# The lag between two lanes of a megakernel: from almost in step to a third of a turn

## The reference

```
x += tanh(g_xattn[0]) * attention_16_heads(layernorm(x), ctx)            # A0
x += tanh(g_ffn[0])   * moe_8_experts_top2_plus_2_shared(layernorm(x))   # M0
x += tanh(g_xattn[1]) * attention_16_heads(layernorm(x), ctx)            # A1
x += tanh(g_ffn[1])   * switch_head_attention(layernorm(x))              # SW, 16 heads, 8 value experts, top 2
x += tanh(g_xattn[2]) * mlstm(layernorm(x), ctx, ctx)                    # ML, 4 heads
x += tanh(g_ffn[2])   * bitlinear_conv_ffn(layernorm(x))                 # CF, 512 hidden
x += tanh(g_xattn[3]) * attention_1_head_with_ffn(layernorm(x), ctx)     # WA
x += tanh(g_ffn[3])   * moe_16_experts_top4_plus_shared(layernorm(x))    # M3
```

## Time and profile before

| what | value |
|---|---|
| median of 3 runs | 2666.93 us (2659.13 to 2669.15) |
| profiled execution, its own time | 2663.77 us |
| its span, first to last instruction | 2661.8 us |
| mean granted TensorE clock | 0.975 |
| PE, DVE, ACT, POOL busy | 89%, 60%, 54%, 5% of the span |
| instructions | 53043 |
| DMA | 115.28 MB, mean 43 GB/s |

### The profile page before, as it was taken

The page is one execution under the profiler, slowest core; times in us unless marked ns, Lnnn a source line. Parts: engine busy times, 40 slices in busy tenths (PEclk is TensorE's granted clock), DMA queues, the critical chain, the costliest instruction groups (busy, mean ns, idle before and its releaser), DMA issues.

```text
span 2661.8 us, 53043 instructions
## 1 busy us (share of the span) xinstructions
PE 2380.6 (89%) x20418; PEld 1673.0 (63%) x20418; DVE 1597.2 (60%) x5337; ACT 1448.7 (54%) x4482; POOL 140.6 (5%) x180
## 2 busy tenths in 40 slices
PE   5999889998899989999899998999889998899998
PEld 3667556675566755667565775557665576665766
DVE  3754766546666475664755657556475565755656
ACT  4376364763647536475455744558345583455833
POOL 0000100001000010000000000000000000000010
PEclk9999999999999999999999999999999999999999
DMA  3024000340003300043000420005200051000510
GB/s 153 1 62 115 9 13 1 76 101 17 5 1 89 88 17 5 1 102 75 17 5 1 112 65 17 5 1 113 63 17 5 1 131 46 18 3 6 141 30 5
DMA packets 312299, 115.28 MB, mean 43 GB/s; under 512 B 268736, under 2 KB 295360, under 8 KB 311792
## 3 DMA queue, kind: packets, MB, share of 16 engines
q1 hardware_dynamic: 312048, 111.90, 16.7%
HBM read 63.64 MB, written 48.23 MB: 42 GB/s over the span
## 4 chain that ended last, share of the span: by engine, by line
PE 52%; DVE 22%; ACT 16%; issue 5%; DMA 3%; POOL 2%; SPq 0%; DVEq 0%; ACTq 0%
ACT PP L821 7%; PE banks L463 5%; PE banks L344 4%; PE banks L407 4%; PE banks L293 3%; PE banks L503 3%; PE banks L574 2%; ACT PP L829 2%; PE banks L341 2%; PE banks L680 2%; DVE nm L1165 2%; PE banks L355 2%; DVE qk L1236 1%; PE banks L456 1%; PE banks L547 1%
## 5 line engine op out<-in xcount | busy, mean ns | idle before, releaser
L821 ACT ACTIVATE PP<-banks,nm 128x128 f32<-128x128 f32 x1568 | 495.7, 419 | 138.8 <-DVE nm L1165 96.1
L1165 DVE TENSOR_REDUCE nm<-banks 128x4 f32<-128x512 f32 (+1 forms) x400 | 261.4, 675 | 323.9 <-PE banks L344 279.2
L293 PE MATMUL banks<-identb 128*128 128x256 bf16 x2112 | 339.6, 277 | 19.1 <-ACT PP L829 15.6
L293 PEld LDWEIGHTS banks<-identb 128*128 128x128 bf16 x2112 | 195.7, 100 | 130.2 <-ACT PP L829 53.9
L407 PE MATMUL banks<-w_sb,PP 128*128 128x128 f32 x1536 | 243.5, 283 | 37.1 <-ACT PP L829 22.4
L829 ACT ACTIVATE PP<-banks 128x512 f32<-128x512 f32 (+1 forms) x400 | 250.9, 638 | 46.9 <-PE banks L407 31.6
L1684 POOL TENSOR_TENSOR mv<-mv,half 128x2 f32<-128x2 f32 x160 | 112.4, 702 | 2339.5 <-DVE mv L1062 2339.5
L407 PEld LDWEIGHTS banks<-w_sb,PP 128*128 128x128 f32 x1536 | 173.0, 143 | 87.8 <-ACT PP L829 49.7
L463 PE MATMUL banks<-w_sb,qk 128*128 128x128 f32 x1280 | 190.8, 287 | 9.0 <-ACT qk L1043 9.0
L463 PEld LDWEIGHTS banks<-w_sb,qk 128*128 128x128 f32 x1280 | 161.1, 191 | 38.1 <-issue 11.4
L812 ACT ACTIVATE xnT<-banks 128x256 f32<-128x256 f32 x128 | 49.1, 384 | 211.4 <-PE banks L301 211.4
(11 more groups left out here) (281 smaller groups left out, 4408.9 us busy)
## 6 DMA issues: line engine op xcount, KB each, us to landing
va<-v_d SPq DMA_DIRECT2D x32, 512.0 KB, 4.8
o_d<-oa SPq DMA_DIRECT2D x64, 256.0 KB, 3.3
va<-o_d SPq DMA_DIRECT2D x32, 512.0 KB, 4.5
pv_d<-PP SPq DMA_DIRECT2D x32, 256.0 KB, 2.0
oa<-pv_d SPq DMA_DIRECT2D x32, 256.0 KB, 3.3
v_d<-PP SPq DMA_DIRECT2D x16, 512.0 KB, 3.8
v_d<-tmp SPq DMA_DIRECT2D x16, 512.0 KB, 6.2
w_sb<-weights SPq DMA_DIRECT2D x1, 5603.0 KB, 23.6
```

Source lines behind the costliest of these rows:

```text
L293: pe.matmul(bank(k, n)[:, cols(c, T)], identb[:, :], bc(identb[:, :], 1, G), start=True, stop=True, skip_group_check=True)
L821: e = act.activation(P[k][:, 512 * (u % 2) + 128 * j:][:, 0:128], bank_[:, cols(j)], ACT.Exp, bias=nm[k][:, m:m + 1], accum_out=ssum[k][:, ...
L1165: e = dve.tensor_reduce(m, b3(scores[:, 0:maps * 128], maps), AX.X, ALU.max, negate=True)
```

## The change

TURN goes from 36496 to 34943 and SHIFT from 1318 to 11636: the keys of lane 1 lie 0.333 of a turn behind lane 0's, where they were 0.036 behind. All five lists of beats and the list of spares have new values; their lengths are the same. The sum of the spares goes from 132 to 212, the entries that aren't zero from 39 to 48, and the largest from 8 to 15. The beats of SyncE now run from -31436 to 692. Of the lists of PE and ACT the first two rows are shown.

```diff
--- before.py
+++ after.py
@@ -34,49 +34,49 @@
 A0, M0, A1, SW, ML, CF, WA, M3 = range(8)
 
 
-TURN, SHIFT = 36496, 1318
+TURN, SHIFT = 34943, 11636
 BEATS_PE = (
-    -398, 99, 355, 606, 918, 1233, 1233, 1786, 2057, 2088, 2276, 2372, 2720, 2741, 3250, 3264, 3271, 3435, 3831, 3923, 3923,
-    3923, 4446, 4727, 4831, 4831, 4939, 5512, 5780, 5780, 5780, 5885, 6047, 6158, 6220, 6327, 6444, 6798, 7066, 7301, 7484,
...
+    -262, 372, 372, 1316, 1447, 1889, 2018, 2182, 2238, 2442, 2657, 2657, 2707, 2743, 2743, 3178, 3442, 3737, 3922, 3986,
+    3996, 4036, 4066, 4348, 4410, 4474, 4576, 4826, 4826, 4826, 5060, 5632, 6143, 6143, 6547, 6910, 6976, 7097, 7119, 7324,
...
 BEATS_ACT = (
-    -80, -80, -80, 205, 616, 662, 1324, 1324, 1324, 1796, 2178, 2483, 2483, 2483, 2752, 3172, 3172, 3339, 3511, 4116, 4245,
-    4621, 5108, 5283, 5681, 5724, 5782, 5792, 5792, 6169, 6358, 6509, 6591, 6747, 7220, 9035, 9225, 9460, 9618, 9717, 9903,
...
+    438, 1172, 1216, 1587, 1596, 1706, 2102, 2121, 2264, 2264, 2421, 2421, 2480, 2480, 2684, 3263, 3673, 3673, 3956, 3956,
+    4204, 4204, 4893, 4943, 4984, 4984, 5121, 5260, 5260, 5913, 5913, 6499, 6536, 6646, 8122, 8955, 8968, 9376, 9483, 9483,
...
 BEATS_DVE = (
-    -1050, -180, -180, 486, 658, 1436, 1436, 2572, 2592, 3007, 3599, 4639, 4765, 5192, 5192, 5254, 5932, 5998, 6096, 6126,
-    6126, 6285, 6360, 6360, 6428, 6542, 6542, 6679, 6972, 6972, 6972, 6972, 6972, 6972, 6972, 7211, 7250, 7895, 7895, 7895,
-    7895, 7895, 8032, 8077, 8330, 8636, 8768, 9040, 9196, 9466, 9556, 10430, 10636, 10966, 11150, 11982, 12252, 13019,
-    13337, 13694, 13694, 14180, 14180, 14180, 14180, 14180, 14180, 14180, 14180, 14180, 14180, 14180, 14578, 14981, 14981,
-    15393, 15602, 15776, 16374, 16575, 16946, 17050, 17050, 17087, 17125, 17218, 17428, 17510, 17605, 17758, 17800, 17800,
-    17800, 18210, 18298, 18453, 18464, 18583, 18583, 18583, 19143, 19162, 19681, 19738, 20426, 20459, 20641, 22259, 22553,
-    23220, 23488, 23672, 23709, 23804, 24103, 24542, 24664, 24664, 24862, 25392, 25548, 25639, 26058, 26179, 27284, 27605,
-    27639, 27712, 28230, 28230, 28272, 28390, 28436, 28911, 29245, 29245, 29587, 29762, 29977, 31316, 31997, 32051, 32158,
-    32664, 32816, 33291, 33408, 33408, 33408, 33468, 33488, 33547, 33798, 34058, 34185, 34313, 34324, 34621, 34908, 34983,
-    35032, 35080, 35217, 35300, 35492, 35539, 36135,)
+    -1150, -262, -262, 355, 377, 1449, 1607, 1810, 1911, 2843, 2908, 3494, 3719, 3752, 3843, 4237, 4915, 4947, 5088, 5147,
+    5147, 5210, 5356, 5412, 5439, 5439, 5445, 5844, 5901, 6138, 6138, 6221, 6524, 6524, 6543, 6543, 6808, 6848, 6848, 7013,
+    7026, 7180, 7358, 7358, 7384, 7557, 7900, 7951, 8741, 9416, 9426, 9714, 9820, 10833, 10936, 11552, 11761, 12264, 12264,
+    12800, 12985, 13181, 14026, 14111, 14144, 14345, 14345, 14345, 14367, 14714, 14714, 14780, 14780, 14780, 14780, 14780,
+    14910, 15664, 16356, 16426, 16489, 16845, 16913, 16915, 17011, 17092, 17156, 17424, 17424, 17440, 17440, 17440, 17472,
+    17472, 17608, 18133, 18434, 18728, 18824, 19115, 19268, 19818, 20375, 20375, 20707, 20887, 20961, 22660, 23017, 23017,
+    23259, 23523, 23523, 23523, 23538, 24321, 24321, 24616, 24964, 25071, 25166, 25479, 25904, 25904, 26527, 26786, 26786,
+    26786, 26935, 26963, 28052, 28054, 28054, 28357, 28510, 28546, 28747, 29899, 29914, 30799, 30999, 31135, 31201, 32195,
+    32461, 32461, 32577, 32584, 32584, 32735, 32834, 32834, 32956, 33016, 33027, 33483, 33483, 33483, 33483, 33666, 33666,
+    33794, 33794, 34096, 34228, 34228, 34838,)
 BEATS_POOL = (
-    18722, 24380, 28829, 30432, 32719, 39274, 39274, 40884, 48435, 51418, 51418,)
+    10737, 15710, 20937, 23950, 33078, 38899, 38899, 39481, 41966, 41966, 42819,)
 BEATS_SP = (
-    -1480, -1399, -1060, -350, -315, -286, -176, -176, -176, 339, 2027, 9598, 9598, 9598, 16957, 22521, 25900, 25900, 25932,
-    25985, 31624, 33101,)
+    -31436, -30075, -28882, -28875, -28698, -28533, -28097, -27805, -27805, -27805, -27805, -27805, -27805, -27752, -26858,
+    -25660, -25626, -22221, -20014, -19970, -13396, 692,)
 
 SPARES = (
-    0, 0, 0, 0, 2, 1, 0, 2, 0, 0, 0, 0, 1, 0, 0, 7, 0, 0, 0, 3, 4, 7, 0, 0, 2, 2, 0, 0, 1, 0, 1, 0, 0, 0, 0, 0, 3, 0, 0, 0,
-    1, 0, 2, 0, 0, 0, 0, 0, 6, 1, 5, 0, 5, 0, 0, 0, 1, 0, 0, 0, 2, 0, 0, 0, 8, 0, 0, 0, 0, 0, 5, 5, 0, 5, 0, 0, 1, 0, 8, 3,
-    0, 7, 0, 8, 0, 0, 1, 3, 0, 2, 5, 0, 4, 0, 1, 0, 0, 3, 2, 2, 0,)
+    2, 1, 3, 2, 7, 0, 6, 1, 2, 0, 10, 0, 1, 0, 0, 0, 0, 1, 0, 3, 4, 3, 9, 3, 15, 0, 4, 7, 0, 0, 12, 0, 0, 0, 0, 0, 0, 0, 0,
+    0, 0, 4, 0, 0, 0, 0, 0, 3, 2, 0, 0, 0, 4, 0, 0, 0, 0, 0, 1, 0, 1, 0, 0, 0, 1, 3, 0, 0, 0, 0, 0, 1, 0, 5, 0, 13, 0, 0, 5,
+    3, 0, 0, 3, 10, 0, 4, 5, 1, 3, 2, 4, 3, 0, 2, 5, 1, 0, 15, 3, 9, 0,)
 
 
 XN_A0, XN_M0, XN_A1, XN_SW, XN_ML, XN_CF, XN_WA, XN_WA2, XN_M3 = range(9)
```

## The result

The changed kernel takes 2749.97 us (median, 2747.96 to 2750.26) against 2664.28 us for the kernel before, measured beside it: a ratio of 1.032, 95% interval 1.0298 to 1.0343. It is slower by 3.2%. I had forecast 2618 us, and the range ended at 2695.

A forecast was written before the change was run, and what follows sets the result against it. No single engine was taken to bound the kernel; the chain hops between them. Setup 28.5, head 70.5, tail 96, 7.667 turns of 315 and end 2.4 gave a 2612 us span, 2618 us measured time; range 2515 to 2695.

The forecast's parts named there:

- The steady turn: One turn of both lanes in the middle of the run: 315 us, against 327.5 before.
- The beats are something like times: Old stage ends follow their listed beats within 11 us, so the new turn of 34943 units would be 313.6 us.
- A full loop beside a thin stage runs without queueing: Attention loops paired with the other lane's thin stages; a gain the collision count does not see, reason for leaning towards 313.6.
- The collision count: Time both lanes want one engine: 88 us per turn in step, 83 a third apart; turn 322, or 319 with the clock.
- The spares: Unread TensorE matmuls ahead of waits: 17.4 us more queue per turn, bounds 0 to 17.4, taken as 0.
- Rival (b): Spares have no gaps on TensorE, so slower: 2685 us half exposed, 2751 all exposed; chance 0.19.
- A lane alone: One lane's eight stages without the other lane sum to 213 to 251 us.
- Head and tail: Lane 0 runs its first third alone, 70.5 us; lane 1 its last, ML to M3, 96 us (bounds 77 and 115).
- Rival (c): Head and tail run at a cold TensorE clock: 2651 us, at worst 2683; chance 0.07.
- ScalarE's share: Sign that the forecast is right: ScalarE busy above 0.57 in every third of a turn.
- The break-even at a turn of 321.5 us: The steady turn's length at which the change would neither gain nor lose.
- Rival (a): The thirds collide as the in-step lanes did: turn 320 us, 2656 us in all, no change; chance 0.15.

The follow-up runs named there:

- h2: Kernel before, without the row sums that ScalarE's exponential accumulates in the switched attention: 2672.9 us, ratio 1.0023.
- e5: Changed kernel with lane 1 eight turns behind, so one lane runs after the other: 4546 us.
- h1: Changed kernel with lane 1 eight turns behind and every group of spares doubled: 4388 us.

## Why the prediction was wrong

*The steady turn: 315 us forecast, 331.1 measured.* This is the step that failed, and 16.1 us in 7 2/3 turns are 123 of the 132 us between 2618 and 2750. Both of its supports failed.

- "The beats are something like times": the new list asked 34.6 us for the first attention and got 46.8 (668.2 to 715.0, lane 0's stage ends). That is 12 of the 16.5 us by which this turn was longer than the 313.4 that the list asked; the other stages took 34.6, 48.2, 93.9, 28.4, 22.8, 27.4 and 27.8. Old ends within 11 us of old beats did not show that the new ones would be met.
- "A full loop beside a thin stage runs without queueing": it saves nothing, because a lane's loop takes 24 to 28 us already in step. Occupied time (81 and 90% of ScalarE) was read as a bound, in windows where two loops overlap; h2 shows for the one at 90% that it is none. For the one at 81% the evidence is the timelines alone.
- The collision count, 5 us a turn and 3 more for the clock (319), was the better estimate, and still too good. Spares at 31% of their time put 5.4 us on the new turn, and 331.1 - 5.4 is 2.3 us under the old. This last is worked out, not run: no kernel has the new order, the clock and the old number. How much of the missing gain is the lanes' own chains and how much the fit of the new order stays open.

*The spares: 0 of 17.4 us taken,* since TensorE had idle time enough in the sum of a turn. The sum does not say that the idle time lies where the spares stand. Measured 31%, 5.4 us a turn. Rival (b) named the right term and the wrong share: with a turn of 331 it would have had to be all of it. Its "all exposed, 2751" agrees with the measured time by accident.

*A lane alone: 213 to 251 us forecast; 272 to 282 measured,* at clocks of 0.86 and 0.74. I had taken the other lane's ScalarE time off each attention (30.5, 32.1 and 50.7 us); e5 has 43.3, 43.0 and 71.1, and h1, at clocks of 0.96, 0.87 and 0.83, has 38.3, 39.8 and 69.0. So a part of the excess is the clock. The rest I put down to the same error as above: the work of the other lane had stood in gaps.

*Head and tail.* Together 166.5 us forecast. The tail was 89.3 (forecast 96, within my bounds). The first turn was forecast at 28.5 + 70.5 + 2/3 of 315 = 309 us and ended at 336.7; 11 of the 28 us missing are the longer turn, and most of the rest is what lane 0 does alone: A0, M0 and A1 ended at 64.7, 95.2 and 136.4 us, where the forecast's stage times after 28.5 us give 59.0, 81.7 and 113.8 (lane 1 is beside it in the later half of A1). Rival (c), the cold ends, is partly there: in the tail the clock is at 0.70 to 0.86, yet ML to M3 took no more than forecast. By the rule of the Trainium skill's page "TensorE: Matmul & The Clock Gate" (section "HAM oscillation — how this bites in real kernels") they would, as I read it, be cold throughout; the tail's windows, 0.96 to 0.70, agree in part.

*What held.* The clock's gain came (0.97 to 0.99) and the drops in A1, ML and M3 are nearly gone. ScalarE's share did not come: forecast above 0.57 in every third of a turn, it is 54.5 of 113 us in the first (668 to 781). SyncE's and GpSimd's new orders cost nothing that I found; the tables stay at 32 loads, of which 8 moved into the loops of line 821 (groups by line of the changed kernel, beside the earlier trace rows):

```profile
L973 ACT ACT_TABLE_LOAD x16 | 20.5, 1283 | 0.3
L821 ACT ACT_TABLE_LOAD x8 | 10.3, 1283 | 0.1
L980 ACT ACT_TABLE_LOAD x8 | 10.3, 1283 | 0.1
```

The break-even at a turn of 321.5 us was right in kind: with the ends fixed, the turn had to fall by 2%, and it rose by 1%.

*Rival (a),* collisions as before (turn 320, 2656 us), was the nearest in mechanism. It had left out the spares' share and the longer head, and with the spares' share taken off the turn is still 5.7 us over its 320.

## What to carry to other kernels

A software lag between two lanes is paid once, in head and tail: here 61 us for a third of a turn, 2.3% of eight turns. It must come back in every turn, so work out the ends first and ask what gain per turn breaks even.

An engine at 80 to 90% in a stretch where two lanes' loops overlap need not be the bound: here each lane's own chain took as long in step as beside another stage, and taking work off the engine in the 90% loop gained nothing. Look at one lane's start-to-start time before taking the other lane's work off.

Filler that holds the clock belongs to one order of the instructions. Change its length and its places with the order, and vary both before the order itself is judged.

## What the runs showed of the hardware that I had not expected

- The filler matmuls are worth 177 us in one order and 281 us in the other (6.6% and 10%), at a price of 31% of their own time while the clock holds.
- With a lane alone, twice the fillers made the kernel faster: 4546 to 4388 us, with the clock from 0.737 to 0.856.
- A lane's loop of eight groups took 24 and 26 us with both lanes in it, and 27 us with the other lane in mLSTM.
- The merged order is fragile: keys taken from the measured start of each chunk, which keep the order within a lane, made the same kernels 6 and 14% slower.
